# Product-key queries by token halves, early query and router weights, and routers with stationary weights

## The reference, cut to what matters

```python
# L1: product keys
q = (x @ Wq).reshape(b, t, H=4, 2, 64);  q1, q2 = q[..., 0, :], q[..., 1, :]
sim1 = einsum('bthd,hkd->bthk', q1, keys[:, :, 0]);  sim2 likewise     # 128 keys a side
s1, i1 = top_k(sim1, 8);  s2, i2 = top_k(sim2, 8)
final, at = top_k(all 64 sums s1[i] + s2[j], 8)                        # of 32 x 128 experts
out = sum over the 8 of silu(x . e_down[expert]) * relu(final) * e_up[expert], over 4 heads
# L2: 8 experts, 2 a token
logits = x @ w_gate;  top, idx = top_k(logits, 2);  weights = softmax(top)
# L3: the same with a shared expert and its gate: 9 columns, softmax over the 8 experts
```

## Time and profile before

| | before |
|---|---|
| three runs | 3241.6, 3245.09 (median), 3249.32 us |
| profiled execution | 3237.14 us |
| its span, first to last instruction | 3235.4 us |
| mean granted TensorE clock | 0.919 |
| TensorE, VectorE, ScalarE, GpSimd busy | 84%, 54%, 36%, 28% |
| HBM read, written | 142.74 MB, 30.67 MB |

### The profile page before, as it was taken

One profiled execution on the slowest core, in us unless ns is written; L12 is line 12 of the kernel. 1 busy time (PEld: TensorE's weight loads), 2 busy tenths in 40 slices (PEclk: granted clock), 3 DMA queues, 4 the chain that ended last, 5 costly groups with the idle time before them and its releaser, 6 DMA issues. The chain is left out here.

```text
span 3235.4 us, 35884 instructions
## 1 busy us (share of the span) xinstructions
PE 2717.5 (84%) x11495; PEld 1664.0 (51%) x11495; DVE 1732.8 (54%) x3048; ACT 1173.5 (36%) x2506; POOL 918.6 (28%) x436
## 2 busy tenths in 40 slices
PE   7998797999764599999699988588689988699895
PEld 3555585644232366665454543366455543577563
DVE  2454675577657899893655653412555653344212
ACT  0111221466615788780144444111134443221110
POOL 0000000488231010100056663122256663222112
PEclk9989898999986799999799998689799998699998
DMA  5220222432100100100332120422432120212613
GB/s 222 81 95 23 72 78 80 96 73 59 53 30 0 53 27 27 52 27 13 103 70 62 38 60 17 182 100 90 141 70 58 42 59 17 78 39 92 214 66 113
DMA packets 101257, 232.26 MB, mean 72 GB/s; under 512 B 22512, under 2 KB 27120, under 8 KB 99696
## 3 DMA queue, kind: packets, MB, share of 16 engines
q1 hardware_dynamic: 88624, 189.46, 19.5%
q0 software_dynamic: 12480, 40.90, 3.8%
HBM read 142.74 MB, written 30.67 MB: 54 GB/s over the span
## 5 line engine op out<-in xcount | busy, mean ns | idle before, releaser
L1534 POOL TENSOR_TENSOR L_attn_total<-L_attn_total,L_attn_probs 128x2048 f32<-128x2048 f32 x120 | 546.4, 4553 | 155.9 <-ACT L_attn_probs L1489 151.3
L1568 DVE TENSOR_REDUCE L_attn_row_max<-L_attn_rows_ps 128x1 f32<-128x512 f32 x512 | 336.0, 684 | 270.2 <-PE L_attn_rows_ps L1374 267.2
L1489 ACT ACTIVATE L_attn_probs<-L_attn_s_ps 128x512 f32<-128x512 f32 x512 | 292.6, 596 | 422.1 <-PE L_attn_s_ps L1394 418.1
L1394 PE MATMUL L_attn_s_ps<-L_attn_q_stack,L_attn_k_stack 98*128 98x512 f32 (+1 forms) x768 | 379.9, 531 | 39.4 <-DMA L_attn_q_stack<-L_attn_ml 33.7
L465 PE MATMUL L_ffn_hidden<-L_ffn_x_high,L_ffn_up_high 128*128 128x512 f32 x688 | 296.1, 430 | 100.3 <-DVE L_ffn_routes L381 53.8
L347 ACT ACTIVATE L_ffn_sums<-sims 128x128 f32<-128x128 f32 x1024 | 315.5, 389 | 50.1 <-DVE L_ffn_routes L360 25.9
L1534 POOL TENSOR_TENSOR L_attn_total<-L_attn_probs 128x2048 f32<-128x2048 f32 x20 | 91.0, 4550 | 796.6 <-ACT L_attn_probs L1489 796.6
L1394 PEld LDWEIGHTS L_attn_s_ps<-L_attn_q_stack,L_attn_k_stack 98*128 98x128 f32 (+1 forms) x768 | 142.8, 195 | 264.1 <-issue 128.5
L465 PE MATMUL L_ffn_hidden<-L_ffn_x_low,L_ffn_up_high 128*128 128x512 f32 x688 | 273.8, 398 | 0.0
L1374 PE MATMUL L_attn_rows_ps<-L_attn_k_stack,L_attn_q_stack 96*128 96x512 f32 x512 | 209.4, 444 | 29.1 <-DVE L_attn_row_max L1568 26.9
L1407 PE MATMUL L_attn_o_ps<-L_attn_probs,L_attn_values 128*32 128x512 f32 x1536 | 210.6, 621 | 26.9 <-ACT L_attn_probs L1489 22.9
(11 more groups left out here) (273 smaller groups left out, 4242.4 us busy)
## 6 DMA issues: line engine op xcount, KB each, us to landing
L_attn_k_stack<-L_attn_kh SPq DMA_DIRECT2D x192, 128.0 KB, 2.4
L_attn_ctxT<-in_ctxT SPq DMA_DIRECT2D x8, 2048.0 KB, 10.7
L_attn_abs_in<-in_L_ffn_w SPq DMA_DIRECT2D x12, 1024.0 KB, 8.3
L_attn_k_stack<-L_attn_kl SPq DMA_DIRECT2D x96, 128.0 KB, 2.4
L_attn_q_stack<-L_attn_qh SPq DMA_DIRECT2D x192, 64.0 KB, 2.0
L_ffn_xg<-x_slots POOLq DMA_DIRECT2D x46, 256.0 KB, 3.2
y_slots<-L_ffn_y_sb POOLq DMA_DIRECT2D x46, 256.0 KB, 2.3
L_ffn_up_all<-in_L_ffn_w SPq DMA_DIRECT2D x16, 704.0 KB, 12.2
```

What stands on the lines that cost most here:

```text
L1394: nc.tensor.matmul(s_ps[:, v % S_SLOTS, :], k_stack[0:depth, n % 2, h, kt * P:(kt + 1) * P], q_stack[0:depth, n % 2, h, :], start=True, st ...
L1489: nc.scalar.activation(probs[:, g % P_SLOTS, h, :], s_ps[:, v % S_SLOTS, :], ACT.Exp, **kinds).then_inc(exp_done, 1)
L1534: nc.gpsimd.tensor_tensor(total[:], first, probs[:, g % P_SLOTS], ALU.add).then_inc(added, 1)
L1568: nc.vector.tensor_reduce(row_max[:, r // HALVES_K, r % HALVES_K:r % HALVES_K + 1], rows_ps[:, r % R_SLOTS, :], AX_X, ALU.max, negate=True ...
```

## The change

- L1: `wq` gets its room and its transfer ahead: SP issues it at the start of the norm block. The queries go by token halves: the four heads of half 0, then those of half 1 with the similarities of tiles 0 and 1 between them. ScalarE copies in the same order.
- L2 and L3: the router is loaded from the norm block too, and the logits are made at the end of the norm block's TensorE stream: the router is the stationary operand (8 or 9 columns) and 512 tokens of `xT` stream, four products a half. They lie as rows of experts, in two PSUM banks. In the expert block ScalarE copies each half out and TensorE turns it, one small transpose a tile.

```diff
 def norm_block(env, name, ..., early_loads=None, router=None):
+            elif early_loads:
+                @block.sync
+                def _(sp):
+                    early_loads(sp)
 ...
                         last = nc.tensor.transpose(turned[:, t % 4, c, :], xn[...], env.ident[:])
                     last.then_inc(transposed, 1)
+                if router:
+                    pe.wait_ge(router.router_loaded, 16)
+                    for h in range(HALVES):
+                        pe.wait_ge(copied, (h + 1) * (TILES // HALVES))
+                        for c in range(DC):
+                            last = nc.tensor.matmul(router.logits_ps[0:router.N, h, :], router.router[:, c, :],
+                                                    env.xT[:, c, h * HALF:(h + 1) * HALF], start=(c == 0), stop=(c == DC - 1))
+                        last.then_inc(router.logits_made, 1)
 ...
 def expert_weights_block(env, name, shared, normalise, gate, weight, first, slots):
-                sp.dma_start(w[:], io["router"]).then_inc(loaded, 16)
                 first["sync"](sp)
 ...
-                pe.wait_ge(loaded, 16)
                 for t in range(TILES):
-                    for i in range(DC):
-                        last = nc.tensor.matmul(ps[:, t, 0:N], env.xT[:, i, t * P:(t + 1) * P], w[:, i, :],
-                                                start=(i == 0), stop=(i == DC - 1))
+                    pe.wait_ge(rows_copied, t // (TILES // HALVES) + 1)
+                    last = nc.tensor.transpose(ps[:, t, 0:N], logits_T[:, t * P:(t + 1) * P], env.ident[0:N, 0:N])
                 last.then_inc(logits_done, 1)
 ...
             def _(act):
+                for h in range(HALVES):
+                    act.wait_ge(slots.logits_made, h + 1)
+                    nc.scalar.copy(logits_T[:, h * HALF:(h + 1) * HALF], slots.logits_ps[0:N, h, :]).then_inc(rows_copied, 1)
                 first["scalar"](act)
 ...
 def product_keys_block(env, name, sims, bar, extra, G, first, query_weights):
-                sp.dma_start(wq[:], io["wq"]).then_inc(wq_loaded, 16)
                 sp.wait_ge(keys_clear, 1)
 ...
+                def query(n):
+                    h, f = n // H, n % H
                     # the four products of head f and half h, as before
+                def similarities(t):
+                    if t % (TILES // HALVES) == 0:
+                        pe.wait_ge(q_done, H * (t // (TILES // HALVES) + 1))
                     # the four products of tile t, as before
+                pe.wait_ge(wq_loaded, 16)
+                for n in range(H):
+                    query(n)
+                pe.wait_ge(keys_loaded, 32)
+                for n in range(H):
+                    query(H + n)
+                    if n in (0, 2):
+                        similarities(n // 2)
+                for t in range(2, TILES):
+                    similarities(t)
 ...
             def _(act):
+                for n in range(H):
+                    query(n)
                 for t in range(TILES):
+                    for n in ((0,), (1, 2), (3,))[t] if t < 3 else ():
+                        query(H + n)
                     act.wait_ge(sims_psum, t + 1)
 ...
                 def score_keys(first):
+                    with nc.sbuf_tensor("L1_ffn_wq", [P, DC, D], F32) as wq:
+                        def load_queries(sp):
+                            sp.dma_start(wq[:], env.io["wq"]).then_inc(wq_loaded, 16)
+                        with x_hat("L1_ffn", x_parts, load_queries):
+                            product_keys_block(env, "L1_ffn", sims, bar, extra, G, first, (wq, wq_loaded))
```

More of the change, by code:

```diff
@@ L119, in finish, with norm_block @@
         dve.wait_ge(self.var_done, TILES)
-def norm_block(env, name, split=None, quantised=False, load_context=None, rows=None):
+def norm_block(env, name, split=None, quantised=False, load_context=None, rows=None, early_loads=None, router=None):
     nc = env.nc
@@ L677, with __init__ @@
 class Slots:
-    def __init__(self, env, name, local):
+    def __init__(self, env, name, local, N):
         nc = env.nc
@@ L685, in sb @@
             return local.enter_context(nc.sbuf_tensor(f"{name}_{n}", shape, dt))
+        self.router, self.N = sb("router", [P, DC, N]), N
         self.rows = sb("rows", [P, TILES, D])
@@ L691, in __init__, with load_router @@
         self.placed, self.scattered = env.sem("placed"), env.sem("scattered")
+        self.router_loaded, self.logits_made = env.sem("router_loaded"), env.sem("logits_made")
         self.up_loaded = [env.sem(f"up_loaded{e}") for e in range(EXPERTS)]
         self.down_loaded = [env.sem(f"down_loaded{e}") for e in range(EXPERTS)]
+    def load_router(self, env, sp):
+        sp.dma_start(self.router[:], env.io["router"]).then_inc(self.router_loaded, 16)
     def scatter(self, env, pool):
@@ L709, in expert_weights_block @@
     N = EX + (1 if shared else 0)
-    loaded, logits_done, step, exp_done = env.sem("loaded"), env.sem("logits_done"), env.sem("step"), env.sem("exp_done")
+    rows_copied, logits_done, step, exp_done = env.sem("rows_copied"), env.sem("logits_done"), env.sem("step"), env.sem("exp_done")
     chosen, ranked, counting, ones_made = env.sem("chosen"), env.sem("ranked"), env.sem("counting"), env.sem("ones_made")
@@ L715, in sb @@
             return local.enter_context(nc.sbuf_tensor(f"{name}_{n}", shape, dt))
-        w = sb("router", [P, DC, N])
+        logits_T = sb("logits_T", [N, TOK])
         logits, top, index = sb("logits", [P, TILES, N]), sb("top", [P, TILES, 8]), sb("index", [P, TILES, 8], U32)
@@ L1037, in _, with product_keys_block @@
                     env.tile_stats.finish(dve)
-def product_keys_block(env, name, sims, bar, extra, G, first):
+def product_keys_block(env, name, sims, bar, extra, G, first, query_weights):
     nc, io = env.nc, env.io
@@ L1053, in sb @@
             return local.enter_context(nc.sbuf_tensor(f"{name}_{n}", shape, dt))
[L1055 removed]
+        keys, qT = sb("keys", [P, H, 2 * NK]), sb("qT", [P, H, TOK])
         full = sb("full", [P, 2, H, 2 * NK])
@@ L1091, in _, with query @@
                     last.then_inc(sims_psum, 1)
+                pe.wait_ge(wq_loaded, 16)
[8 more added lines that the diff above has]
+                    similarities(t)
             @block.scalar
             def _(act):
-                for n in range(H * HALVES):
-                    f, h = n // HALVES, n % HALVES
+                def query(n):
+                    h, f = n // H, n % H
                     act.wait_ge(q_psum, n + 1)
                     nc.scalar.copy(qT[:, f, h * HALF:(h + 1) * HALF], q_ps[:, n % 4, :]).then_inc(q_done, 1)
+                for n in range(H):
+                    query(n)
                 for t in range(TILES):
+                    for n in ((0,), (1, 2), (3,))[t] if t < 3 else ():
+                        query(H + n)
                     act.wait_ge(sims_psum, t + 1)
@@ L2189, in x_hat @@
         @contextmanager
-        def x_hat(name, x_parts):
+        def x_hat(name, x_parts, early_loads=None):
             with nc.sbuf_tensor(f"{name}_xT", [P, DC, TOK], F32) as env.xT:
-                norm_block(env, name, split=x_parts)
+                norm_block(env, name, split=x_parts, early_loads=early_loads)
                 yield
@@ L2202, in expert_layer @@
                 full = E // P
-                slots = Slots(env, name, local)
+                slots = Slots(env, name, local, EXPERTS + (1 if shared else 0))
                 def up_tile():
@@ L2236, in route @@
                         def route(first):
-                            with nc.sbuf_tensor(f"{name}_xT", [P, DC, TOK], F32) as env.xT:
-                                norm_block(env, name, split=x_parts, rows=slots.rows)
+                            with nc.sbuf_tensor(f"{name}_xT", [P, DC, TOK], F32) as env.xT, \
+                                    nc.psum_tensor(f"{name}_logits_ps", [P, HALVES, HALF], F32) as slots.logits_ps:
+                                norm_block(env, name, split=x_parts, rows=slots.rows, router=slots,
+                                           early_loads=lambda sp: slots.load_router(env, sp))
                                 expert_weights_block(env, name, shared, normalise, gate, weight, first, slots)
@@ L2253, in load_all @@
                             load_down(sp, down_sb, e)
-                    with nc.sbuf_tensor(f"{name}_xT", [P, DC, TOK], F32) as env.xT:
-                        norm_block(env, name, rows=slots.rows)
+                    with nc.sbuf_tensor(f"{name}_xT", [P, DC, TOK], F32) as env.xT, \
+                            nc.psum_tensor(f"{name}_logits_ps", [P, HALVES, HALF], F32) as slots.logits_ps:
+                        norm_block(env, name, rows=slots.rows, router=slots,
+                                   early_loads=lambda sp: slots.load_router(env, sp))
                         expert_weights_block(env, name, shared, normalise, gate, None,
@@ L2286, in score_keys @@
```

(9 more changed lines are left out.)

9 lines of the change are left out of this document (2 added, 7 removed).

## The result

The changed kernel took 3227.43 us (median of 5 runs, 3212.89 to 3229.51) beside 3243.35 us for the kernel before on the same chip: a ratio of 0.9941, 95% interval 0.9922 to 0.9960. So it saves 16 to 21 us by the medians, 18 to 19 by the ratios. The profiled execution took 3227.43 us with a span of 3225.7, only 9.7 us under that of before. Why one profile shows so much less than the medians is the first thing to explain.

The account below looks back on a forecast made before the run. The kernel was taken as a sum of stages, since engines meet at every block's end, with VectorE the bound in L1 from tile 1 on. Savings of 8.9 + 11.4 + 0 = 20.3 us off 3245.09 gave 3225 us, range 3213 to 3236.

Parts of the forecast that it names:

- Part 1: L1, early `wq` and queries by token halves: tile 3 reaches VectorE at 1004.7 against 1013.63 us, saving 8.9 us.
- The slow start of the stream: L1's queries on TensorE: 4.4 us at half rate before the full clock, costing 2.2 us.
- The stall: L1, tile 0's routes: a VectorE operation is held while GpSimd makes the rest of the weights, taken as 4.5 us.
- its upper end: L1 without a stall of VectorE beside GpSimd: a saving of 13.4 us.
- Part 2: L3, logits made inside the norm: VectorE gets them at 2780.0 instead of 2791.44 us, saving 11.4 us.
- the block's end behind TensorE: L3's norm block: its end waits for TensorE's last products, 2777.8 us, where the other engines need until 2775.1.
- the shared expert's weights arrive while VectorE still ranks: L3: SP's weights for the shared expert come 2 us later, inside the 9 us that VectorE still ranks.
- Part 3: L2, logits made inside the norm: logits and scatter 7.1 us earlier, first slot tile at 2115.7 against 2115.88; saves nothing.
- the mechanism named: L2: expert weights start at 2071.0 instead of 2065.07 us, so the scatter shares transfers with them to the end.
- The rival that L2 keeps its 7 us: L2: the scatter is bound by its issue, not its share, so 7.1 us stay; 27.4 saved, 3217.7 us; chance 0.15.
- The sum: Whole kernel: 8.9 + 11.4 + 0 = 20.3 us saved, 3225 us expected; chance of the forecast 0.70.
- The low clock: Two rivals: L2 and L3 logits products at 0.50, 3238 us, chance 0.10; L1's queries too, 3263 us, chance 0.05.

Follow-up runs that it names:

- all weights early: The changed kernel with all of L2's expert weights issued behind the router in the norm's block; 3216.70 us, ratio 0.9937 to the kernel before.
- half early: The changed kernel with the weights of L2's first four experts issued behind the router in the norm's block; 3206.77 us, ratio 0.9906 to the kernel before.
- the half without it: Kernels holding only the changed L1 queries (3233.52 us, ratio 0.9972) or only the changed L2 and L3 routers (3230.65 us, 0.9968), against the kernel before.

## Why the prediction was right

- *Part 1, 8.9 us.* Right. TensorE's start was forecast at 12.9 us after the square root and came at 12.8, tile 1 at 44.0 and came at 44.6, tile 3 at 65.0 and came at 65.4: 8.6 saved. The slow start of the stream cost more than the 2.2 us taken: TensorE's granted clock was 0.50 for the first 6 us, where 4.4 were taken, and 1.00 from there, and the first group's copy came 6.6 us after its start where a group takes 3.45. The stall was put at 4.5 and was 4.3; without it the part gives 4.3 more, as its upper end had it.
- *Part 2, 11.4 us.* The mechanism is right, including the block's end behind TensorE. The logits were forecast 17.05 us after the square root and came at 16.4. Of the 12.1 us that this gives, 10.3 arrive at the shared expert's first product (27.7 us after the square root, before 38.0) and 8.6 at the stage's end in this pair of profiles, 11.5 in the mean below. The forecast let the shared expert's weights arrive while VectorE still ranks and put that at no cost. By the rows of L3 after (2.27 us for 0.48) it cost 1.8: the ranking now meets GpSimd's split of these weights, which had been done before while VectorE waited for the logits. No run took this meeting out. Where the other 1.7 us up to the stage's end went was not tried.
- *Part 3, nothing.* Right, by the mechanism named: scatter 7.9 us earlier, weights 14.9 us after the square root instead of 9.2, first slot tile 1.1 us earlier. In the scatter's first 8 us the queues moved

```profile
q1 hardware_dynamic: 832, 2.32, 81.0%
q0 software_dynamic: 185, 0.63, 19.2%
```

as in the earlier trace rows (packets, MB), and from 2078 to 2105 us the scatter had 4.20 MB of 10.87: after the start it got 3.57 of the other 7.92, nearly half, as forecast. But the first 8 us, whose share the forecast took as it stood, are two things. Read in halves (2078 to 2082 us, the first row, and 2082 to 2086) they are

```profile
q1 hardware_dynamic: 538, 1.49, 101.7%
q1 hardware_dynamic: 294, 0.83, 60.2%
q0 software_dynamic: 185, 0.63, 38.5%
```

The scatter, first issued at 2078.04, moves nothing until 2083 and from then on nearly half of all bytes. Before the change, too, it moves nothing from 2089 to 2093. With all weights early, where they are nearly through when the scatter begins, its first packet comes within 2 us. The Trainium skill ("DMA: Bandwidth & Descriptors", section "Queues, rings and completion order") has each DMA engine go round its queues, a packet at a time. From the scatter's first packet on the trace agrees, with 0.63 MB beside 0.83 and then 3.57 beside 4.36; why that packet comes 4 to 6 us after the issue beside a busy queue no run here shows. The rival that L2 keeps its 7 us fell with the same rows, and half early shows its price: its stage takes 223.7 us, those of the five kernels with L2 as changed 230.4 in the mean, 6.7 more.
- *The sum.* 20.3 us forecast. The table's means, over the kernels that hold a part in the change's form against the kernel before and the half without it, give 9.7, 1.1 and 11.5 us: 22. The last rests on two references that lie 5 us apart (472.5 and 477.6); against before alone L3 gives 9. The first pair of profiles gives 17.3 for the three stages. Measured were 15.9 and 21.0 by the medians, so the runs cannot tell the forecast's 20.3 from 16.
- *The low clock.* Neither rival on it came: the products ran at granted clock 1.00 and 0.45 us a record in L3, 1.00 and 0.44 in L2; the queries had 0.50 for 6 us only.

What the forecast did not say is that an execution's attention stages move by 4.5 us between two profiles of one kernel and by 10.6 over all kernels, as much as a part is worth, so that one profile's difference, 9.7 us, is no measure of this change.

## What to carry to other kernels

Move a transfer and the work behind it as one: what starts earlier on one engine was worth 1 us of 7.9 in L2, where its competitor for transfers started later, and a block that takes on work holds up every queue that waits for its end. When a stage gets shorter, look which background operation of GpSimd its VectorE work now meets. Compare stages bounded by the same event in both traces before the spans.

## Not expected of the hardware

- SyncE issued twelve transfers of 512 KB in 6 us, and the 13th and 14th then took 2.8 to 4.2 us in five kernels that issue all 24 in a row, the one before the change among them (3.3): an issue is then no cheap step, and it holds its block open.
- A scatter issued by GpSimd beside a busy queue of SyncE had its first packet 4 to 6 us after its first issue in five kernels, and within 2 us in the one where SyncE's transfers were nearly through.
- A stall between VectorE and GpSimd does not need large operations: 128x64 elements, 0.48 us for two, took 2.27 beside GpSimd's 2.57.
- TensorE's mean clock over the same 2016 records of L2's attention was 0.91 and 0.92 in two executions of one kernel, 4.6 us apart.
